# A four-layer graph network: the first layer's degrees taken from row sums on VectorE, its linear layer issued one graph ahead

## The reference

```python
h = relu(layernorm(x))
A = adj + eye
deg = A.sum(axis=-1)
dis = where(isinf(deg ** -0.5), 0, deg ** -0.5)
A_hat = dis[:, :, None] * A * dis[:, None, :]
out = A_hat @ (h @ W.T + b)
# batch norm over all 32 * 512 nodes, then relu, then + res_weight * h
```

## Time and profile before

| what | value |
|---|---|
| median of three runs | 4201.18 us |
| the profiled execution, its own time | 4210.96 us |
| its span in the profile | 4209.2 us |
| mean granted TensorE clock | 0.957 of full speed |
| PE busy | 3866.0 us, 92% of the span |
| DVE busy | 3196.1 us, 76% |
| ACT busy | 2031.6 us, 48% |
| POOL busy | 1437.5 us, 34% |
| all DMA | 307.52 MB, mean 73 GB/s |

### The profile page before, as it was taken

How to read it: one execution, slowest core, us unless ns; L and a number is a source line. 1 busy time by engine, 2 the same in 40 slices (tenths; PEclk the granted TensorE clock), 3 DMA queues, 4 the chain that set the end, 5 groups by cost and what they waited for, 6 DMA issues and landing times.

```text
span 4209.2 us, 59912 instructions
## 1 busy us (share of the span) xinstructions
PE 3866.0 (92%) x19682; PEld 2750.9 (65%) x19682; DVE 3196.1 (76%) x5252; ACT 2031.6 (48%) x3078; POOL 1437.5 (34%) x853
## 2 busy tenths in 40 slices
PE   6999857999999999999999999999999999999986
PEld 4777634666666666666666666666666666666665
DVE  4555456788888888888888888888888888888753
ACT  3555424555555444555555455555555455545430
POOL 3444423333333333333333333333333333333310
PEclk9999968999999999999999999999999999999985
DMA  5555422222222222222222222222212222222200
GB/s 175 173 174 173 145 60 60 61 66 65 65 65 65 65 65 65 65 65 65 65 65 58 62 60 65 65 64 60 58 49 58 55 62 65 65 65 65 56 15 10
DMA packets 227165, 307.52 MB, mean 73 GB/s; under 512 B 27184, under 2 KB 128432, under 8 KB 227120
## 3 DMA queue, kind: packets, MB, share of 16 engines
q1 hardware_dynamic: 227120, 306.94, 26.2%
HBM read 155.33 MB, written 50.33 MB: 49 GB/s over the span
## 4 chain that ended last, share of the span: by engine, by line
PE 71%; DVE 14%; issue 8%; ACT 3%; POOL 3%; SPq 0%; DMA 0%; DVEq 0%; POOLq 0%; ACTq 0%
PE bank L1384 11%; PE obank L1318 10%; PE bank L1245 9%; PE bank L1438 8%; PE pair L1245 7%; PE bank L1346 6%; PE pair L1302 6%; PE bank L1403 3%; PE pair L1279 3%; DVE rden L965 2%; DVE diag L1015 2%; PE pair L1151 2%; PE bank L1420 1%; DVE minus_max L957 1%; PE obank L1331 1%
## 5 line engine op out<-in xcount | busy, mean ns | idle before, releaser
L624 ACT ACTIVATE pT<-pair 128x1024 f32<-128x1024 f32 x512 | 511.2, 1027 | 457.0 <-PE obank L1318 271.4
L542 POOL TENSOR_TENSOR pT<-pT,node_edge 128x1024 f32<-128x1024 f32 x256 | 576.1, 2250 | 252.0 <-ACT pT L624 249.8
L957 DVE TENSOR_REDUCE minus_max<-pair 128x2 f32<-128x1024 f32 x512 | 608.7, 1217 | 52.7 <-PE pair L1279 49.2
L1438 PEld LDWEIGHTS bank<-v,p3T 128*128 128x128 f32 x4096 | 505.1, 199 | 43.6 <-DVE p3T L1098 32.6
L1438 PE MATMUL bank<-v,p3T 128*128 128x65 f32 x4096 | 506.8, 280 | 19.8 <-DVE p3T L1098 19.8
L1318 PE MATMUL obank<-pT,v 128*64 128x512 f32 x2048 | 488.0, 608 | 9.4 <-ACT rden L677 4.4
L1384 PE MATMUL bank<-w_s,hid 128*128 128x256 f32 x2048 | 478.9, 388 | 1.2 <-DVE hid L1031 1.1
L947 DVE TENSOR_TENSOR pT<-pT,node_edge 128x1024 f32<-128x1024 f32 x256 | 382.1, 1502 | 109.8 <-ACT pT L624 109.7
L487 POOL TENSOR_TENSOR d_rs<-d_ve,minus_half 128x4 f32<-128x4 f32 x32 | 32.2, 1008 | 1265.7 <-DVE d_ve L804 1265.7
L1384 PEld LDWEIGHTS bank<-w_s,hid 128*128 128x128 f32 x2048 | 382.0, 191 | 86.0 <-issue 36.3
L1245 PE MATMUL bank<-hT,w_s 128*128 128x512 f32 x1536 | 403.5, 401 | 1.4 <-issue 1.0
(11 more groups left out here) (188 smaller groups left out, 6551.2 us busy)
## 6 DMA issues: line engine op xcount, KB each, us to landing
pT<-in_adjT SPq DMA_DIRECT2D x32, 1024.0 KB, 5.1
q_parts<-high_parts SPq DMA_DIRECT2D x256, 128.0 KB, 2.4
a_at<-in_adjT SPq DMA_DIRECT2D x64, 512.0 KB, 3.4
k_parts<-high_parts SPq DMA_DIRECT2D x256, 128.0 KB, 5.6
b_at<-in_adjT SPq DMA_DIRECT2D x64, 512.0 KB, 6.8
hid<-in_x SPq DMA_DIRECT2D x32, 512.0 KB, 4.1
x_res<-hid SPq DMA_DIRECT2D x32, 512.0 KB, 3.2
pre_bn<-hsq SPq DMA_DIRECT2D x32, 512.0 KB, 4.6
```

What stands on the lines that cost most here:

```text
L542: nc.gpsimd.tensor_tensor(half, half, node_edge[:, 0:2, :], ALU.mult).then_inc(a_masked[0].sem, 1)
L624: nc.scalar.activation(dst, pair[p][:, :, :], func, **more).then_inc(a_copied[p].sem, 1)
L957: nc.vector.tensor_reduce(minus_max[:, t, 2 * two_heads:2 * two_heads + 2], pair[p][:, :, :], AX.X, ALU.max, negate=True).then_inc(a_copie ...
L1438: i = nc.tensor.matmul(dst[:, t * w:(t + 1) * w], p3T[:, k, t * P:(t + 1) * P], v3[:, k * H3 + h, :], start=k == 0, stop=k == T - 1)
```

## The change

`degrees` no longer reads a product of TensorE. The adjacency is loaded a second time, not transposed (new kernel input `adj`, new part `load_nat`, two DMAs of 512 KB per graph into two buffers `c_nat`), and DVE sums its rows. `degree_rows`, `degree_columns` and `copy_rows` are gone. `c_hs` has two buffers, and `lin`, `bias_lin` and `scale_lin` work one graph further ahead; `turn`, `copy_hT`, `norm`, `c_stats` and `residual` do as well; the order of the parts is another on every engine. The split of the weights moves ahead of the first pass, because `c_nat` takes the memory in which the raw weights lie. The pass takes two steps more to fill.

```diff
+        c_hs = [[a_xbo[:, 2 * q:2 * q + 2, :] for q in range(2)],
+                [diag[...]..., row_buf[...]...]]
+        c_nat = [[att1T[:, :, :], a_at[:, :, :]], [... for t in (a_o, x_mid)]]
-            for n in range(-2, 2):
+            for n in range(-4, 2):
...
+            def load_nat(g, par):
+                if not g.below(2):
+                    sp.wait_ge(*c_deg_sum.upto(g.plus(-1), 0))
+                elif first(g):
+                    sp.wait_ge(w_low.sem, 5)
+                for q in range(2):
+                    sp.dma_start(c_nat[par][q], nodes(adj, g)[:, 2 * q:2 * q + 2, :]).then_inc(c_nat_in[par].sem, 16)
-            first_pass(sp, [(2, load_x), (1, load_at), (-1, store_o), (1, store_res)])
+            first_pass(sp, [(1, load_at), (2, load_nat), (-1, store_o), (4, load_x), (2, store_res)])
...
 def degree_power
+                if not g.below(2):
+                    pool.wait_ge(*c_o_ok.upto(g.plus(-1), 0))
                 nc.gpsimd.tensor_tensor(c_dis[:, par, :], c_deg[:, 3, :], c_deg[:, 2, :], ALU.mult).then_inc(c_dis_ok.sem, 1)
-            first_pass(pool, [(-1, add_o), (-1, add_sq), (2, lambda g, par: rstd("c", g)), (1, degree_power)])
+            first_pass(pool, [(3, lambda g, par: rstd("c", g)), (1, degree_power), (-1, add_o), (-1, add_sq)])
...
-            first_pass(act, [(-1, scale_o), (0, scale_lin), (1, copy_hT), (-1, square), (2, norm), (1, copy_rows)])
+            first_pass(act, [(-1, scale_o), (-1, square), (1, scale_lin), (2, copy_hT), (3, norm)])
...
 def degrees
+                dve.wait_ge(*c_nat_in[par].upto(g.half(), 2))
+                if not first(g):
+                    dve.wait_ge(*c_dis_ok.upto(g, 0))
+                for q in range(2):
+                    i = nc.vector.tensor_reduce(c_deg[:, 1, 2 * q:2 * q + 2], c_nat[par][q], AX.X, ALU.add)
+                i.then_inc(c_deg_sum.sem, 1)
                 dve.wait_ge(*c_deg_sum.upto(g, 1))
-                nc.vector.tensor_scalar(c_deg[:, 0, :], bank[0][:, 0:T], 0.0, None, ALU.is_equal).then_inc(c_deg_in.sem, 1)
+                nc.vector.tensor_scalar(c_deg[:, 0, :], c_deg[:, 1, :], 1.0, 0.0, ALU.add, ALU.is_equal).then_inc(c_deg_in.sem, 1)
...
-            first_pass(dve, [(0, bias_lin), (1, residual), (1, eye), (2, c_stats), (2, lambda g, par: shift("c", g)),
-                             (1, degrees)])
+            first_pass(dve, [(3, c_stats), (2, residual), (1, degrees), (1, bias_lin), (3, lambda g, par: shift("c", g)),
+                             (1, eye)])
...
-            first_pass(pe, [(0, lin), (1, turn), (1, first_degrees), (0, aggregate)])
+            first_pass(pe, [(1, lin), (2, turn), (0, aggregate)])
```

More of the change, by code:

```diff
@@ L93, in gnn_stack @@
 def gnn_stack(nc, x, adjT, w0T, b0, bn_w, bn_b, res_w, wqT, wkT, wvT, woT, bo, eps, w1, b1, rms_w, w2, b2,
-              w3, att, out):
+              w3, att, adj, out):
     f32, bf16, f32r = mybir.dt.float32, mybir.dt.bfloat16, mybir.dt.float32r
@@ L141, in gnn_stack @@
         bnw_s, bnb_s = bn_c[:, 5, :], bn_c[:, 6, :]
-        row_part = sb("row_part", P, 1)
         ln = {s: {n: sb(f"{s}_{n}", P, T, w) for n, w in (("st", 6), ("mv", 2), ("ve", 1), ("rs", 1), ("sh", 1))}
@@ L209, in gnn_stack @@
         c_o, c_sq = two(hsq, 0, 4), two(p3T, 0, 4)
-        c_h, c_hT, c_hs = a_h, b_at[:, K:2 * K, :], a_xbo
+        c_h, c_hT = a_h, b_at[:, K:2 * K, :]
+        c_hs = [[a_xbo[:, 2 * q:2 * q + 2, :] for q in range(2)],
+                [diag[:, :, :].rearrange("p (b c) n -> p b (c n)", b=2), row_buf[:, :].rearrange("p (b d) -> p b d", b=2)]]
+        c_nat = [[att1T[:, :, :], a_at[:, :, :]],
+                 [t[:, :, :].rearrange("p (k b) d -> p k (b d)", k=2) for t in (a_o, x_mid)]]
         sum_o, sum_sq = x3, b_at[:, 0:K, :].rearrange("p k (b d) -> p (k b) d", d=D)
@@ L238, in gnn_stack @@
         c_biased = signal("c_biased", 2)
-        c_row_sum = signal("c_row_sum")
-        c_row_ok = signal("c_row_ok")
+        c_nat_in = [signal(f"c_nat_in{i}", 2, 16) for i in range(2)]
         c_hs_ok = signal("c_hs_ok")
@@ L336, in step @@
                         part(g, (par + ahead) % 2)
-            for n in range(-2, 2):
+            for n in range(-4, 2):
                 step(Graph(n), n % 2)
-            with eng.Fori(1, G // 2 - 1) as i:
+            with eng.Fori(1, G // 2 - 2) as i:
                 for o in range(2):
                     step(Graph(i, o, 2), o)
-            for n in range(G - 2, G + 1):
+            for n in range(G - 4, G + 1):
                 step(Graph(n), n % 2)
@@ L397, in load_a @@
             def load_a(g):
-                if first(g):
-                    sp.wait_ge(w_low.sem, 5)
-                else:
+                if not first(g):
                     sp.wait_ge(*lns["a"]["h"].upto(g, 0))
@@ L482, in _ @@
                                     pattern=[[-1, P]], channel_multiplier=1).then_inc(consts.sem, 1)
-            nc.gpsimd.memset(row_part[:, :], 1.0 / ROW_LOW).then_inc(consts.sem, 1)
-            pool.wait_ge(consts.sem, 16)
+            pool.wait_ge(consts.sem, 15)
             def power(out_ap, in_ap, n):
@@ L570, in normalise @@
                 i.then_inc(lns[s]["h"].sem, 1)
+            act.wait_ge(weights_in.sem, n_loads * 16)
+            for w, src in zip((wq_s, wk_s, wv_s), raw):
+                nc.scalar.activation(w[:, 0], src, ACT.Copy).then_inc(w_high.sem, 1)
+            for k in range(K):
+                nc.scalar.activation(w1_s[:, 0, k], raw1[k], ACT.Copy).then_inc(w_high.sem, 1)
             def norm(g, par):
@@ L602, in scale_lin @@
                     for t in (2 * q, 2 * q + 1):
-                        i = nc.scalar.activation(c_hs[:, t, :], c_hs[:, t, :], ACT.Copy, scale=c_dis[:, par, t:t + 1])
+                        i = nc.scalar.activation(c_hs[par][q][:, t % 2, :], c_hs[par][q][:, t % 2, :], ACT.Copy, scale=c_dis[:, par, t:t + 1])
                 i.then_inc(c_hs_ok.sem, 1)
[L606 to L611, removed]
-            first_pass(act, [(-1, scale_o), (0, scale_lin), (1, copy_hT), (-1, square), (2, norm), (1, copy_rows)])
[L615 to L618, removed]
+            first_pass(act, [(-1, scale_o), (-1, square), (1, scale_lin), (2, copy_hT), (3, norm)])
             def a_take(g, u, dst, func=ACT.Copy, **more):
@@ L763, in _ @@
             dve.wait_ge(weights_in.sem, n_loads * 16)
-            dve.wait_ge(consts.sem, 16)
+            dve.wait_ge(consts.sem, 15)
             nc.vector.tensor_scalar(eps_ident[:, :], ident[:, :], eps_s[:, 0:1], None, ALU.mult).then_inc(setup.sem, 1)
@@ L783, in _ @@
                     n += 2
+            for n, (w, src) in enumerate([(w, raw[i]) for i, w in enumerate((wq_s, wk_s, wv_s))]
+                                         + [(w1_s[:, :, k], raw1[k]) for k in range(K)]):
+                dve.wait_ge(w_high.sem, n + 1)
+                nc.vector.tensor_tensor(w[:, 1], src, w[:, 0].bitcast(f32), ALU.subtract).then_inc(w_low.sem, 1)
             def stats(s, g, src):
@@ L827, in degrees @@
             def degrees(g, par):
-                dve.wait_ge(*c_deg_sum.upto(g, 1))
+                dve.wait_ge(*c_nat_in[par].upto(g.half(), 2))
                 if not first(g):
                     dve.wait_ge(*c_dis_ok.upto(g, 0))
-                nc.vector.tensor_scalar(c_deg[:, 0, :], bank[0][:, 0:T], 0.0, None, ALU.is_equal).then_inc(c_deg_in.sem, 1)
+                for q in range(2):
+                    i = nc.vector.tensor_reduce(c_deg[:, 1, 2 * q:2 * q + 2], c_nat[par][q], AX.X, ALU.add)
+                i.then_inc(c_deg_sum.sem, 1)
+                dve.wait_ge(*c_deg_sum.upto(g, 1))
+                nc.vector.tensor_scalar(c_deg[:, 0, :], c_deg[:, 1, :], 1.0, 0.0, ALU.add, ALU.is_equal).then_inc(c_deg_in.sem, 1)
                 dve.wait_ge(*c_deg_in.upto(g, 1))
                 nc.vector.tensor_scalar(c_deg[:, 2, :], c_deg[:, 0, :], -1.0, 1.0, ALU.mult, ALU.add).then_inc(c_deg_in.sem, 1)
-                nc.vector.tensor_tensor(c_deg[:, 1, :], bank[0][:, 0:T], c_deg[:, 0, :], ALU.add).then_inc(c_deg_ok.sem, 1)
+                nc.vector.scalar_tensor_tensor(out=c_deg[:, 1, :], in0=c_deg[:, 1, :], scalar=1.0, in1=c_deg[:, 0, :],
+                                               op0=ALU.add, op1=ALU.add).then_inc(c_deg_ok.sem, 1)
             def residual(g, par):
@@ L844, in bias_lin @@
             def bias_lin(g, par):
-                if not first(g):
-                    dve.wait_ge(*c_agg.upto(g, 0))
+                if not g.below(2):
+                    dve.wait_ge(*c_agg.upto(g.plus(-1), 0))
                 for q in range(2):
                     dve.wait_ge(*c_lin.upto(g, q + 1))
-                    nc.vector.tensor_tensor(c_hs[:, 2 * q:2 * q + 2, :], pair[1][:, q, :].rearrange("p (b d) -> p b d", d=D),
+                    nc.vector.tensor_tensor(c_hs[par][q], pair[1][:, q, :].rearrange("p (b d) -> p b d", d=D),
```

(13 more changed lines are left out.)

## The result

The changed kernel takes 4135.56 us (median of 4 runs, 4127.78 to 4136.98) against 4203.36 us for the one before in the same timing; the ratio is 0.983 (95% interval 0.981 to 0.986). Five more rounds of the same two kernels gave 4127.84 against 4207.14 us, ratio 0.9811 (0.9797 to 0.9824), so 68 and 79 us less. The forecast was 48 us less, 4153 us; the direction, the range and the place were right, the gain 1.4 to 1.7 times what the likeliest case said.

A forecast was written before the change was run, and what follows sets the result against it. TensorE and the ACT, DVE, PE chain were taken to bound the first pass together, at 15.08 us. A longer fill, 28 steps of 13.3 us and two shorter, plus 0.46 us at the end, gave 4201 - 48 = 4153 us; range 4112 to 4180.

The forecast's parts named there:

- the likeliest case: First pass: the adds' lock on DVE sets a 13.3 us period, giving 4153 us (4138 to 4170), chance 0.62.
- TensorE's own work: TensorE, first pass: without degree products and waits, 11.9 us per graph remain, the period if nothing else bound it.
- The lock: DVE and GpSimd exclude one another in some operations; taking turns, the adds hold eye, making the period 13.3 us.
- E = D + 7.15: DVE, first pass: eye's end (E) comes 7.1 to 7.2 us after degrees' end (D), held by the adds.
- The chain over `norm`: From degrees' end D through bias_lin, scale_lin, copy_hT to norm at D + 5.6: a limit of 11.7 us per graph.
- the collision: DVE's shift and eye meeting GpSimd's two adds in the first pass; TensorE gets a new wait of about 1.4 us.
- Rival 1: First pass: no collision that counts, period at TensorE's floor of 11.9 us, time about 4113 us; chance 0.20.
- The fill: Start of the first pass: five weight subtractions and more steps put the first aggregation at 60.4 us instead of 48.08.
- The sum: First pass: second aggregation at 72.4, 28 steps of 13.3, two shorter; last aggregation at 466.8 us, 48 us gained overall.
- rival 2: DMA queue, first pass: the added megabyte makes x land late; period 15.8 us would give about 4226 us; chance 0.05.
- Rival 3: First pass: GpSimd keeps the lock through both adds, period 14.7 us, time about 4192 us, no change; chance 0.08.
- rival 4: First pass stays at 15 us for an unseen wait and the longer fill is lost: 4201 to 4212 us; chance 0.05.

The follow-up runs named there:

- e5: Changed kernel with copy_hT and norm ahead of scale_lin on ACT and add_o ahead of degree_power on GpSimd: 4098.29 us (median of 5), ratio 0.9732 to the kernel before.
- e1: Changed kernel with GpSimd's two adds (add_o, add_sq) cut to one column per tile: 4117.68 us, period 12.45 us.
- e2: Changed kernel with two of the four scalings of scale_lin left out: 4127.11 us, period 12.41 us.
- e3: Changed kernel with both the adds cut to one column per tile and half of scale_lin left out: 4105.51 us, period 11.62 us.
- e8: Changed kernel with the second copy of the adjacency loaded for the first two graphs only: 4122.96 us, period 12.45 us.
- e11: Changed kernel with add_o moved ahead of degree_power on GpSimd, ACT's order untouched: 4148.95 us, period 13.20 us.
- e6: Changed kernel with both adds ahead of degree_power on GpSimd, ACT's order untouched: 4206.91 us, period 15.28 us.
- e7: Changed kernel with one c_hs buffer, bias_lin waiting for the previous graph's aggregation: 4246.71 us, period 16.69 us, in six of thirty 15.01.

## Why the prediction was right, and where its sizes were off

- **The work that goes.** Both degree products and their wait, 2.3 us, went, and the wait for the scaled output too.
- **TensorE's own work** was put at 11.9 us; e5 shows 11.23. I had added up starts across the old aggregation, which held the gaps around `degree_rows`; in one piece 32 products take 6.90 us, not 7.27. The rest is small: from start to start the transposes take 0.88 us, not their row's 1.04, and the linear layer 3.45, not 3.54.
- **The reductions** take 1.21 us each, and from the start of the statistics to the end of `degrees` it is 309.24 - 303.14 = 6.10 us, the 6.1 of the sum.
- **The lock** is where the first size was off. Of E = D + 7.15 the trace shows 6.4: the adds end at D + 6.25 as forecast (6.1), but two pieces of `eye` get in ahead of `add_o`, not none or one, and only one is left behind `add_sq`, which then needs 0.15 us, not 0.7. By itself this brings 13.3 down to 12.5.
- **The chain over `norm`** is the step whose reasoning failed. The prediction gave "D + 5.6, so 11.7, under TensorE's floor" for the pass without the collision. It let `scale_lin` start behind the bias and forgot that it waits for GpSimd's `c_dis` too, at D + 1.54. So both halves of `scale_lin`, 1.6 us from D + 1.65 to the start of `copy_hT` at D + 3.26, stand behind that wait, and not one half of 0.9. `norm` ends at D + 6.22, and this limit is 12.4 us, as long as the adds' one within what e1 (12.45) and e2 (12.41) tell apart. e1 to e3 show both. That the omission doesn't show in the time is luck: this limit happens to be no longer than the one through the adds. Rival 1, in which the period goes to TensorE's floor when the collision alone doesn't count, was therefore not open in this kernel: e1 stays at 12.45.
- **The fill**: the first aggregation was put at 60.4, it starts at 60.11; the slower phase of TensorE that I took at 3 us is there (6.78 us for the second linear layer, against 3.72 later), and the five subtractions take 4.07 us here (25.23 to 29.30), the 4.1 of the sum.
- **The sum**: the last aggregation was put at 466.8 and starts at 436.56, 30.2 us earlier. The second one starts at 71.34 instead of 72.4 (1.1 us); the 28 steps from it to graph 29's, at 417.37, take 12.36 each on average instead of 13.3 (26.4 us); the last two take 19.2 instead of 22 (2.8 us). So nearly all of the miss is the period.
- **DMA**: 80% was forecast, 82% (100 to 440 us) and 85% (100 to 400) are measured; x takes 5.1 us to land and isn't waited for in this stretch. The period at which rival 2's sum is zero comes out as (514.34 - 72.4 - 22) / 28 = 15.0 and not 14.9; nothing hangs on it. Rival 2 is out for this kernel by e8. Rival 3, GpSimd keeping the pair through both adds, is out by the pieces of `eye`, and rival 4 by the period.

The Trainium skill ("SBUF — State Buffer", section "SBUF: two separate sides") calls the pair that VectorE and GpSimd share an exclusive lock held for the whole instruction. The trace agrees: pieces of `eye` last 2.44 us beside adds of 2.40 and 0.28 without one.

## What to carry to other kernels

When two waits end within 0.2 us of each other, as `eye` and `norm` do here, no single cut can show more than that; cut both, or you will call each of them harmless. When work is moved onto VectorE, look at what GpSimd does just then: two adds in its queue cost `eye` 4.3 us here, which was free only because another chain was as long (e1). And list every semaphore that the moved instruction waits for, not only the one that came last before: the one that was early becomes late.

## What the runs showed of the hardware

Two things I had not expected. A DVE operation with a single SBUF input of 4 columns (L846, `tensor_scalar`) was held to 0.94 and 0.95 us while `add_o` ran in e11 and e5, and its neighbour L848 to 2.27 us beside `add_sq` in e6; both take 0.17 without an add. The reduction of 1024 columns from SBUF, in e5 begun beside the same add (rows below), kept its 1.21. The Trainium skill ("VectorE: DVE Perf Modes", section "The perf-mode tier table (the rule you actually need)") gives `tensor_scalar` on fp32 in SBUF a doubled mode and `tensor_reduce` none, and the Trainium skill ("SBUF — State Buffer", section "SBUF: two separate sides") counts operations in a two-port mode among those that need the shared pair. The rows fit that. They don't show the mode itself, as 4 columns are too few to tell by their duration; the one hint is in the setup, where a `tensor_scalar` of 256 columns (L776) takes 0.35 us and a reduction of 256 (L788) takes 0.42.

```profile
306.39 2.36 POOL L508 TENSOR_TENSOR x<-x,hsq 128x1024 f32<-128x1024 f32 x1
306.58 1.21 DVE L843 TENSOR_REDUCE c_deg<-x_mid 128x2 f32<-128x1024 f32 x1
307.83 0.95 DVE L846 TENSOR_SCALAR c_deg<-c_deg 128x4 f32<-128x4 f32 x1
```

The other is the granted clock. In e7 it fell to 0.50 behind most of the waits of 3.5 us, but not behind six of thirty. In e6 the waits before the linear layer alternate: behind those of 2.1 us it takes 3.7 us, behind those of 3.8 us it takes 5.4, with one exception (3.72 us at 278.55). In e11 with 1.7 us of 13.2 and in the kernel before with 0.85 and 0.4 of 15.1 it kept its 3.7 us. So the wait just before the work doesn't decide by itself; what else does isn't shown. In e6 the lower clock cost no time, as the chain over `degrees` set the period: 15.28 us behind a slow linear layer and 15.31 behind a fast one.

In e5 the DMA engines are at 95.6% from 100 to 400 us, and DVE waits for x nine times, 5.6 us in all; that they would be the next limit if TensorE's work got shorter is a guess that no run tests.
